# Second attention: where the turned row maxima stand in the ring of row scores

## What is computed

```python
xn = _layernorm(x, axis=-1)                        # 4 batches of 2048 tokens, width 256
s = _L1_attn_ref(xn, L1_attn_wq, ...)              # 16 heads of width 16
    q, k = _apply_rope(q, k, sin, cos)
    att = jnp.einsum('bhtd,bhsd->bhts', q, k) * scale
    att = jnp.where(causal[None, None], att, -jnp.inf)
    att = jax.nn.softmax(att, axis=-1)
    y = jnp.einsum('bhts,bhsd->bhtd', att, v)
g = _silu(_L1_ffn_ref(xn, ...))                    # 8 experts, top 2
x = x + s * g
```

## Time and profile before

| | |
|---|---|
| median of 3 runs | 3221.84 us (3221.32 to 3222.61) |
| the profiled execution | 3216.31 us, its span 3214.5 us |
| second attention, all groups | 821 to 2306 us of the span |
| one group | 92.85 us (1288.37 to 1381.22) |
| PE, DVE, ACT busy in that group | 88.24, 85.08, 85.05 us |

### The profile page before, as it was taken

The page is one execution under the profiler, slowest core; times in us unless marked ns, Lnnn a source line. Parts: engine busy times, 40 slices in busy tenths (PEclk is TensorE's granted clock), DMA queues, the critical chain, the costliest instruction groups (busy, mean ns, idle before and its releaser), DMA issues. The chain is left out here.

```text
span 3214.5 us, 66525 instructions
## 1 busy us (share of the span) xinstructions
PE 2893.3 (90%) x26519; PEld 1757.1 (55%) x26520; DVE 2555.0 (79%) x3560; ACT 2044.4 (64%) x3430; POOL 674.3 (21%) x1035
## 2 busy tenths in 40 slices
PE   5888888872899999999999999999899999999987
PEld 3555555550334443344344434434388888888975
DVE  4888888877899999999999999999265665666567
ACT  2555555540699999999999999999732232333234
POOL 1333333341222322000000000000132343332300
PEclk9999999985899999999999999999999999999999
DMA  2223333325223112222220122202121222212349
GB/s 76 69 86 89 88 91 93 93 86 102 51 55 54 36 24 54 54 54 53 54 53 17 43 54 54 53 22 87 52 68 34 71 80 73 68 42 70 103 150 309
DMA packets 252583, 230.21 MB, mean 72 GB/s; under 512 B 60908, under 2 KB 234988, under 8 KB 252012
## 3 DMA queue, kind: packets, MB, share of 16 engines
q1 hardware_dynamic: 235896, 192.32, 22.9%
q0 software_dynamic: 16384, 33.64, 3.3%
HBM read 124.21 MB, written 101.06 MB: 70 GB/s over the span
## 5 line engine op out<-in xcount | busy, mean ns | idle before, releaser
L1746 ACT ACTIVATE at_ex<-at_so,keep_exp_scale 128x512 f32<-128x512 f32 (+1 forms) x2304 | 1336.3, 679 | 203.6 <-PE at_so L1582 115.8
L1784 DVE TENSOR_REDUCE at_best<-at_p 128x2 f32<-128x1024 f32 (+3 forms) x1280 | 1284.5, 1060 | 111.1 <-PE at_p L1602 80.9
L1621 PE MATMUL at_so<-at_qs,at_ks 50*128 50x512 f16 (+3 forms) x2560 | 734.3, 352 | 33.0 <-ACT at_ex L1746 32.6
L1602 PE MATMUL at_p<-at_ks,at_qs 48*128 48x512 f16 (+3 forms) x2560 | 681.4, 358 | 50.6 <-DVE at_best L1784 49.4
L1692 PE MATMUL at_so<-at_ex,at_vs 128*32 128x256 f32 (+2 forms) x8704 | 697.2, 392 | 0.0
L2020 ACT ACTIVATE e_hh<-e_hb,e_b1now 128x512 fp32r<-128x512 f32 x256 | 176.4, 689 | 519.0 <-PE e_hb L1954 504.6
L1621 PEld LDWEIGHTS at_so<-at_qs,at_ks 50*128 50x128 f16 x2560 | 208.2, 93 | 517.6 <-ACT at_ex L1746 339.4
L1257 POOL DMA_INDIRECT e_xg<-s_xn,e_token x128 | 143.4, 1121 | 1359.5 <-DVE e_token L1252 1235.0
L1984 PE MATMUL e_ob<-e_w2h,e_hh 128*128 128x256 f32 x1024 | 295.3, 288 | 15.1 <-DVE e_og L2091 15.1
L1986 PE MATMUL e_ob<-e_w2h,e_hl 128*128 128x256 f32 x1024 | 291.8, 285 | 0.0
L1985 PE MATMUL e_ob<-e_w2l,e_hh 128*128 128x256 f32 x1024 | 291.7, 285 | 0.0
(11 more groups left out here) (267 smaller groups left out, 4498.6 us busy)
## 6 DMA issues: line engine op xcount, KB each, us to landing
s_v<-a_v SPq DMA_DIRECT2D x64, 256.0 KB, 3.0
s_qk<-a_part SPq DMA_DIRECT2D x128, 128.0 KB, 2.4
at_vs<-s_v SPq DMA_DIRECT2D x32, 512.0 KB, 10.3
s_eo<-at_empty SPq DMA_DIRECT2D x16, 1024.0 KB, 7.6
e_w<-w SPq DMA_DIRECT2D x16, 1024.0 KB, 7.7
f_rows<-s_eo SPq DMA_DIRECT2D x32, 512.0 KB, 8.0
at_qs<-s_qk SPq DMA_DIRECT2D x96, 128.0 KB, 4.4
at_ks<-s_qk SPq DMA_DIRECT2D x96, 128.0 KB, 7.2
```

Source lines behind the costliest of these rows:

```text
L1602: last = pe.matmul(out, qs[rows, buf, p, qt * P:(qt + 1) * P], ks[rows, buf, p, ch * SEG:ch * SEG + w], start=True, stop=ch != qc)
L1621: last = pe.matmul(so[:, v % NST, at:at + w], ks[rows, r, p, kt * P:(kt + 1) * P], qs[rows, r, p, q0:q0 + w], start=True, stop=not diag)
L1746: ev.done(act.activation(ex[:, v % NE, 0:width], so[:, v % NST, 0:width], ACT.Exp, scale=keep["exp_scale"][:, 0:1]), "ex")
L1784: last = dve.tensor_reduce(best[:, row:row + PAIRS * TT + 1:PAIRS * TT, ch], p1[:, at % NP1, :, to:to + w], AX, ALU.max)
```

## The change

A turning has no item of its own any more. `stream` hangs it on the last item of a quarter whose columns sum to 256 (`HALF_BANK`): such an item leaves half of each bank free. PE writes the item's scores into columns 0 to 255 and, once both heads' scores and masks are done, the transpose into columns 256 to 383 of the same place (`turn_maxima`); DVE reduces the item and then does the two splitting steps from there (`turn_down`), and only the last of them frees the place. `t` items stay only in `tail`, where their carrier is missing. `lead` goes from 44 to 42 items, `run` from 80 to 76.

The hooks move, since the last narrow item of quarter `qc` is number 4·qc+1 of its quarter and the old `t` stood at number 2:

| turned maxima | item and half-step before | item and half-step now |
|---|---|---|
| quarter 2 | 2, half-step 2 | 15, half-step 14 |
| quarter 3 | 36, half-step 32 | 34, half-step 32 |
| next group's quarter 0 | 43, half-step 38 | 44, half-step 42 |
| next group's quarter 1 | 59, half-step 52 | 63, half-step 59 |

```diff
         def stream(quarters, turned):
             out = []
             for (ahead, qc), t in zip(quarters, turned):
                 chunks = quarter(ahead, qc)
-                out += chunks[:2] + ([("t",) + t] if t else []) + chunks[2:]
+                k = [k for k, x in enumerate(chunks) if sum(w for _, _, _, w in x[4]) == HALF_BANK][-1]
+                out += chunks[:k] + [chunks[k][:5] + (t,)] + chunks[k + 1:]
             return out
...
-                            masked = [("s1", out[:, w - P:w], key_mask, a, i == len(parts) - 1)]
+                            masked = [("s1", out[:, w - P:w], key_mask, a, i == len(parts) - 1 and not (turned and e == 1))]
...
-                def turn_maxima(g, it, n, items, k):
-                    _, ahead, qc = items[k]
-                    at = n + k
-                    if at >= NP1:
-                        ev.wait(pe, "mx", it, at + 1 - NP1)
+                def turn_maxima(g, n, items, k):
+                    if items[k][0] == "c" and not items[k][5]:
+                        return
+                    ahead, qc = items[k][1:] if items[k][0] == "t" else items[k][5]
                     ev.wait(pe, "neg", g + ahead, qc + 1)
-                    pe.transpose(p1[:, at % NP1, 0, 0:P], negmax[:], ident[:]).then_inc(ev.sem["s1"], 2)
+                    turned = pe.transpose(p1[:, (n + k) % NP1, 0, HALF_BANK:HALF_BANK + P], negmax[:], ident[:])
+                    turned.then_inc(ev.sem["s1"], 2 if items[k][0] == "t" else 1)
...
                         if e == 1:
+                            for k in paired:
+                                turn_maxima(g, LEAD, items, k)
                             for k in due_now[1:]:
                                 rows_alone(g, r, use, g, LEAD, items, k)
...
+                        if turned:
+                            turn_down(g + turned[0], turned[1], p1[0:QROWS, at % NP1, 0, HALF_BANK:HALF_BANK + P])
+                            return
                         ev.done(last, "mx")
```

More of the change, by code:

```diff
@@ L1368, in quarter @@
                     banks.append([(qt, qc, 0, (i + 1) * P)])
-                out += [("c", ahead, qc, p, parts) for parts in banks for p in range(PAIRS)]
+                out += [("c", ahead, qc, p, parts, None) for parts in banks for p in range(PAIRS)]
             return out
+        HALF_BANK = 2 * P
         def stream(quarters, turned):
@@ L1390, in slots @@
         def slots(items):
-            work = np.cumsum([sum(w + HW for _, _, _, w in x[4]) if x[0] == "c" else 2 * P for x in items])
+            work = np.cumsum([sum(w + HW for _, _, _, w in x[4]) + (2 * P if x[5] else 0) if x[0] == "c" else 2 * P for x in items])
             return [min(u for u in range(2 * NS) if step_work[u + 1] * work[-1] >= w * step_work[-1]) for w in work]
@@ L1398, in attend_phase @@
         slot_of = [int(u) for u in np.maximum.accumulate([max(u, earliest.get(x[:3], 0)) for u, x in zip(slots(run), run)])]
-        kept = [k for k, x in enumerate(run) if x[0] == "o" or x[1] == 0]
-        tail, tail_slot = [run[k] for k in kept], [slot_of[k] for k in kept]
+        kept = [k for k, x in enumerate(run) if x[0] == "o" or x[1] == 0 or x[5] and x[5][0] == 0]
+        tail = [run[k] if run[k][0] == "o" or run[k][1] == 0 else ("t",) + run[k][5] for k in kept]
+        tail_slot = [slot_of[k] for k in kept]
         LEAD, RUN = len(lead), len(run)
@@ L1410, in turned_at @@
         def turned_at(items, ahead, qc):
-            return items.index(("t", ahead, qc)) + 1
+            return [k for k, x in enumerate(items) if x == ("t", ahead, qc) or x[0] == "c" and x[5] == (ahead, qc)][0] + 1
         def outputs_at(g, qc):
@@ L1587, in open_rows @@
                 def open_rows(r, use, it, n, items, k, e):
-                    _, ahead, qc, p, parts = items[k]
+                    _, ahead, qc, p, parts, turned = items[k]
                     at = n + k
@@ L1592, in open_rows @@
                         ev.wait(pe, "mx", it, at + 1 - NP1)
-                    if ahead == 1 and e == 0 and items[k] == quarter(1, 0)[0]:
+                    if ahead == 1 and e == 0 and items[k][:5] == quarter(1, 0)[0][:5]:
                         ev.wait(pe, f"in{(r + 1) % NBUF}", use, 1)
@@ L1657, in rows_alone @@
                 def rows_alone(g, r, use, it, n, items, k):
-                    if items[k][0] == "t":
-                        turn_maxima(g, it, n, items, k)
-                    elif items[k][0] == "o":
+                    if items[k][0] == "o":
                         turn_outputs(g, n, items, k)
+                    elif items[k][0] == "t":
+                        ev.wait(pe, "mx", it, n + k + 1 - NP1)
+                        turn_maxima(g, n, items, k)
                     else:
                         close(open_rows(r, use, it, n, items, k, 0) + open_rows(r, use, it, n, items, k, 1))
+                        turn_maxima(g, n, items, k)
                 def half_step(g, r, use, s, p, first, items, due_now):
@@ L1774, in normalise, with turn_down @@
                                       ALU.mult).then_inc(ev.sem["mx"], 1)
+                def turn_down(g, qc, src):
+                    ev.wait(dve, "m_in", g, G * PART * qc)
+                    ev.done(dve.tensor_scalar(mT[:, 0], src, 1.0 / LIFT, None, ALU.mult), "mstep")
+                    ev.wait(dve, "mstep", g, qc + 1)
+                    dve.scalar_tensor_tensor(out=mT[:, 1], in0=src, scalar=1.0 / LIFT, in1=mT[:, 0],
+                                             op0=ALU.mult, op1=ALU.subtract).then_inc(ev.sem["mx"], 1)
                 def stream_item(g, it, n, items, k):
@@ L1780, in stream_item @@
                     if item[0] == "c":
-                        _, ahead, qc, p, parts = item
+                        _, ahead, qc, p, parts, turned = item
                         for i, (qt, ch, to, w) in enumerate(parts):
@@ L1793, in stream_item @@
                     else:
[L1794 to L1800, removed]
+                        turn_down(g + item[1], item[2], p1[0:QROWS, at % NP1, 0, HALF_BANK:HALF_BANK + P])
                 def group(g, r, use, first, more):
```

## The result

The changed kernel takes **3389.0 us** (median of 4 runs, 3382.79 to 3393.36), the one before 3221.58 (4 runs, 3220.45 to 3222.61): 1.0518 times as long, 95% interval 1.05 to 1.0537. The forecast was 3378, range 3338 to 3418. The profiled execution took 3387.91, its span is 3386.1.

A forecast was written before the change was run, and what follows sets the result against it. PE was taken to set the pace, with SyncE's in-order queue a second bound. Per group 11.65 stall + 2.15 clock − 1.65 ring = 12.15 us, 158 in groups 1 to 13, +156 in all: 3378 us, range 3338 to 3418.

The forecast's parts named there:

- What bounds: Second attention: PE sets the pace, idling 4.6 us per 92.85 us group; SyncE's in-order queue is a second bound.
- The ring: Ring p1: four items per group lose their own place, gaining 1.65 us per group, between 0.7 and 2.3.
- SP's chain: SyncE's queue: copies of quarter 2's maxima, loads and y output all start 16.9 us later, 15.9 to 17.1.
- The wait for the maxima: PE ahead of quarter 2's keys: the copied maxima come late, costing 0.95 us alone, inside the stall otherwise.
- The landing: Y output lands 18.2 us behind the first load's issue, holding DVE's output 1; PE's half-step 25 runs 11.65 later.
- The clock: PE's clock after the halt: 5 us at the low level, 2.15 us lost per group, bounds none and 3.65.
- The small terms: Groups 0 and 14 at −0.7 us each, group 15 at +0.6, the lead ahead of group 0 about −1.
- The sum: Groups 1 to 13 at 12.15 us each, 158 us; with the other groups and the lead, +156 in total.
- A: Rival: PE stalls but loses no clock, 10.0 us in each of thirteen groups, 3350 us; chance 0.08.
- B: Rival: loads don't hold the y output, so DVE never waits, 3211 us; decides at landing 6.2 behind first load; chance 0.04.
- C: Rival: neither the wait for maxima nor that for the output costs anything, −1.65 us fifteen times, 3197 us; chance 0.02.
- D: Rival: the stall at its worst with 8.3 us at low clock, 17.1 us per group, 3443 us; chance 0.06.

The follow-up runs named there:

- e4: Changed kernel, but quarter 2's maxima have their own item at the old place again, the other turnings ride: 3197.55 us, 0.9918 of the kernel before.
- e6: Kernel before with only quarter 3's maxima riding on a narrow item, on the second chip: 0.999 of the kernel before there.
- e8: Kernel before with only the next group's quarter 1 riding on a narrow item, on the second chip: 0.9983 of the kernel before there.
- e7: Kernel before with only the next group's quarter 0 riding on a narrow item, on the second chip: 0.9971 of the kernel before there.
- e5: Kernel before with only quarter 2's maxima riding and the y output issued ahead of the loads, second chip: 1.0081 of the kernel before there.
- e1: Changed kernel with the previous group's quarter 3 y output issued ahead of the fourteen loads: 3226.93 us, 1.001 of the kernel before.
- e2: Changed kernel with the y output issued behind the twelve 128 KB loads, ahead of the two of 512 KB: 3330.9 us, 1.0342 of the kernel before.
- e3: Kernel before, ring untouched, with only SyncE's copies of quarter 2's maxima waiting for an item fourteen places later: 3400.64 us, 1.0546 of the kernel before.

## Why the prediction held, and where its sizes were off

**What bounds** was read rightly: with PE as the pace, DVE and ACT at 85 of 92.85 us, what PE lost in the ring less shortened the groups (e4, e6 to e8). It isn't all idle time, as the prediction counted: of e4's 1.70 us, 1.07 is idle time of PE (4.61 before, 91.15 − 87.61 = 3.54 there) and 0.63 is less busy time for the same 1144 matmuls.

**The ring.** Predicted 0.35, 0.7, 0.6 and 0 for quarter 3, the next quarters 0 and 1, and quarter 2; measured 0.38, 0.96, 0.36 and, ahead of the wait for the maxima, 0.20 lost. The sum was right (1.65 against 1.70), two of its parts were not: the next quarter 0 came out 0.26 higher and the next quarter 1 0.24 lower, and it is luck that these cancel. The next quarter 0 was worth more than the 0.87 of its three waits in the earlier trace rows, of which 0.17 had been taken off for DVE; comparing the starts of half-steps in e7 with before, 1.07 is gained by half-step 43 and 0.11 given back by 45. For the next quarter 1, in e8, PE is 1.13 ahead at half-step 54, behind the transpose's old place, more than the 0.61 and 0.19; with the transpose in its new place, half-step 59, it is 0.20 ahead, and 0.36 from half-step 60 on. DVE gave 0.77 back, where the step took off 0.2.

**SP's chain.** L1792 was expected 20.50 us into the group (1308.87 − 1288.37) at its end; it ends at 1570.60 + 0.28 − 1550.16 = 20.72. The first load starts 25.68 into the group, 17.1 later than the 8.55 of the earlier trace rows; 16.9 had been said, 17.1 was the upper bound.

**The wait for the maxima**: 0.95 forecast, 0.90 in the row above; half-step 20 starts 1.18 later there than before, 1.13 in e5. The prediction's own terms give 1314.5 − 1313.91 = 0.59, and up to 1.0 more, so its 0.95 was a choice within them. The wait lay inside the stall, as said.

**The landing.** In the group shown, DVE's step at 1593.67 comes 17.8 us behind the first load's issue; over the thirteen groups the output lands 17.67 behind it (16.0 to 19.7), for 18.2 taken from the rows of before. PE's row scores of half-step 25 start at 1594.45 − 1550.16 = 44.29, against 32.68 before: 11.61 late, 11.54 in the mean; 11.65 was forecast.

**The clock** is the term that was mis-sized. 5 us at the low level were taken, 2.15 lost. In group 7 the row scores run 44.29 into the group and the end is at 105.64, 61.35 later; before it was 60.17; with the 1.70 of the ring that makes 2.88 lost. The clock was at its low level from 37.5 to 51.1 us into the group, 6.9 us of it after PE went on: 0.54 in the mean of 1594 to 1602, 1.00 behind. So 42% of the low time was lost, as the 44% from the earlier trace rows said; it was the length, taken near the 4.1 us of one stretch where the work had just come back, that was short. 0.72 a group too little makes 9 us in thirteen groups. The Trainium skill, TensorE: Matmul & The Clock Gate, Terms, puts the loss at half of the throttled time; the trace, with 42%, stays below that, and so do the falls of the last section that no stall precedes (35%).

**The small terms.** Group 14 gained 0.56 for 0.7, group 0 gained 1.86 for 0.7, and group 15 lost 0.28 for 0.6. The lead's −1 can't be seen: group 0 starts at 820.89, before at 820.71, and between 817.7 and 821.6 in e1 to e4.

**The sum** in the two traces: groups 1 to 13 +165.2 (158 forecast), groups 0 and 14 −2.4, group 15 and the lead +0.5, and the stage of the experts, which the change doesn't touch, +8.8:

```profile
2477.50:3263.90 786.40, 763.59 (x4863) 697.29 (x4864) 480.20 (x742) 240.38 (x336) 261.88 (x247) 0.98 0.21 67
```

Before, the same view of that stage gives:

```profile
2314.30:3091.90 777.60, 755.73 (x4863) 690.38 (x4864) 479.71 (x742) 240.01 (x336) 262.67 (x247) 0.99 0.21 68
```

With what lies behind that stage, 171.6 more span; 167.4 between the medians, where 156 was forecast. The profiled execution of the kernel before was 5.3 us shorter than its median, that of the changed one 1.1, so the medians leave some 4 of the 8.8, if the second attention takes the same in every execution. Of the 11 us that the forecast missed, 7 lie in groups 1 to 13, which the clock term covers.

**Rivals.** A, no loss of clock: refuted by the 0.54. B and C, no stall: refuted by thirteen waits; the shortest landing was 16.0 us behind the first load, where B decides at 6.2. The Trainium skill, DMA: Bandwidth & Descriptors, section Queues, rings and completion order, says that completion is not first in, first out per issuing engine; no run here shows an output that gained by it. B's condition, made true by hand in e1, gave 3226.93 and not 3211, so B's own sum missed a cost, mostly the first one of the last section. D: no group reached its 17.1, the longest had 14.7.

## What to carry to other kernels

Moving a step moves every queue that waits for it: before shortening a wait of a tenth of a microsecond, list what the DMA queue has written behind that step and when each of its users is due. A small store that a reused buffer waits for belongs ahead of bulk loads on the same queue; with it there the changed kernel was 162 us shorter. And when one of several like edits moves a producer late, leave that one out: three of a group's four rides keep all of the gain.

## What the runs showed of the hardware that was not expected

**After a wait of 1 us the clock sometimes falls in a PE that is otherwise full.** In e5's group at 1436.85 PE waits 0.87 us ahead of quarter 2's keys, and 2.6 us on the granted clock is at its low level for 6.8 us, with PE busy all the time:

```profile
1463.61 0.39 PE L1631 MATMUL at_so<-at_qs,at_ks 50*128 50x512 f16 x1 [0.87 <-DMA at_qs<-at_mT]
```

```profile
1466.20:1472.90 6.70, 6.70 (x50) 2.46 (x48) 4.08 (x8) 4.56 (x8) 0.00 (x0) 0.50 1.05 198
```

This group lasts 96.38, the next with the same wait of 0.87 lasts 93.98 at a clock of 1.00: 2.40 us are lost, 35% of the low time, and the fall comes in some groups only. On the first chip such a fall, 27 to 31 us into a group, is in 13 of the 45 groups 1 to 15 of the changed kernel, e1 and e2, in 2 of the 15 of e3, and in none of the 30 of the two kernels without the wait (before and e4). All three of the 45 that waited 2.25 us or more fell; of the other 42, with 0.54 to 1.14, ten did. In e3 the two that fell had waited 2.81 and 0.78, and none of the 13 with 0.42 to 0.61 fell. The kernels with the wait are also those with the late loads, whose transfers run in just this stretch (198 GB/s above). That e3 has these loads too speaks for the wait, but no run separates the two, and what decides between two groups with the same wait was not tried.

**A stage with the same code doesn't keep its clock.** The stage of the experts had 3 short stretches at the low level in the trace of before, behind the one with which it starts, and 8 in that of the changed kernel: 17.1 us more low time, 8.8 us longer, about half. In e1 to e4 it lasted 782.3 to 786.5 with 5 to 8 such stretches. It isn't shown whether the change has a part in this, or only the moment at which the stage starts; it is up to 9 us that no count of instructions gives.

**Two chips differ.** On the second chip the kernel before took 3332.04, 111 us more. In the trace of e8 its group 1 (the first line) is slow and group 7 (in the fence of e8 above) is not:

```profile
920.58:1021.52 100.94, 91.99 (x1146) 38.38 (x1142) 85.57 (x101) 86.10 (x148) 28.10 (x52) 1.00 0.20 44
```

Groups 0 to 4 last 96 to 110 us in e5 to e8, group 15 93.7 to 97.9 (88.92 before on the first chip), and the stage of the experts 843.5 to 848.7; groups 5 to 14 are mostly undisturbed. The slow stretches are those in which GpSimd is busy beside the other engines (28.10 us here, none in groups 5 to 14, 7.6 in group 15); on the first chip the same work of GpSimd costs nothing in group 1 (92.86, GpSimd busy 26.37). That is where the difference lies, not its cause, which was not looked for.
